# Second table in eight short steps; gated output projections made three per iteration, early in the attention loop

## The reference, cut to what matters

```python
mod = (silu(c) @ wmod).reshape(16, 6, 1, -1)     # sa, ca, ga, sb, cb, gb
ga, gb = sign(.) * maximum(abs(.), 0.25)
h = layernorm(x) * (1 + ca) + sa
x = x + ga * attention(h)     # 4 heads, two learned-slot tables of 64, causal, gated, then @ Wo
h = layernorm(x) * (1 + cb) + sb
x = x + gb * experts(h)       # layer norm, router, top 2 of 8 experts, 128 -> 512 -> gelu -> 128,
                              # weighted sum of the two, layer norm
```

## Time and profile before

| what | value |
|---|---|
| median of three runs | 498.81 us (498.32 to 500.5) |
| the profiled execution | 499.39 us |
| its span | 497.6 us |
| TensorE busy | 436.6 us, 88% |
| VectorE busy | 398.8 us, 80% |
| GpSimd busy | 347.0 us, 70% |
| ScalarE busy | 316.9 us, 64% |
| chain that ended last | TensorE 49%, GpSimd 23%, VectorE 16% |

### The profile page before, as it was taken

The page is one execution under the profiler, slowest core; times in us unless marked ns, Lnnn a source line. Parts: engine busy times, 40 slices in busy tenths (PEclk is TensorE's granted clock), DMA queues, the critical chain, the costliest instruction groups (busy, mean ns, idle before and its releaser), DMA issues.

```text
span 497.6 us, 11499 instructions
## 1 busy us (share of the span) xinstructions
PE 436.6 (88%) x3266; PEld 363.0 (73%) x3266; DVE 398.8 (80%) x1134; ACT 316.9 (64%) x813; POOL 347.0 (70%) x404
## 2 busy tenths in 40 slices
PE   3589999999899899899899766699889999999990
PEld 1366777776677677677677544599889999999980
DVE  2579999999989989989989975467677677786385
ACT  1166778888578678678688645565545555555574
POOL 4675865689979989989987546267567656665632
PEclk9999999999889889889999958599999999999996
DMA  6950000000000000000000050235434322226344
GB/s 152 236 160 0 7 8 5 2 18 19 25 17 19 23 19 19 24 17 19 24 22 14 18 193 23 54 75 175 148 91 105 90 72 69 73 65 229 118 137 125
DMA packets 33934, 33.66 MB, mean 68 GB/s; under 512 B 7037, under 2 KB 27681, under 8 KB 33745
## 3 DMA queue, kind: packets, MB, share of 16 engines
q1 hardware_dynamic: 27600, 22.39, 16.7%
q0 software_dynamic: 4320, 9.22, 5.5%
q10 hardware_dynamic: 1952, 1.32, 1.1%
HBM read 20.43 MB, written 12.48 MB: 66 GB/s over the span
## 4 chain that ended last, share of the span: by engine, by line
PE 49%; POOL 23%; DVE 16%; issue 6%; ACT 4%; DVEq 1%; DMA 0%; ACTq 0%; POOLq 0%
PE sa_ps L1625 12%; POOL xe_dram L388 8%; PE sa_ps L1635 6%; PE bank L1635 6%; PE sa_ps L1403 3%; POOL lgs L422 3%; POOL A_sb L395 3%; PE bank L1616 2%; POOL xn L473 2%; PE bank L1475 2%; POOL kT L445 2%; PE sa_ps L1396 2%; PE bank L1476 2%; PE bank L1600 2%; PE bank L1542 2%
## 5 line engine op out<-in xcount | busy, mean ns | idle before, releaser
L738 ACT ACTIVATE work<-sa_ps,work 128x128 f32<-128x128 f32 x284 | 81.0, 368 | 63.8 <-PE sa_ps L1625 61.9
L483 POOL DMA_INDIRECT y_dram<-work,idxr x71 | 72.4, 1020 | 44.8 <-DVE idxr L1203 32.4
L388 POOL DMA_INDIRECT xe_dram<-xrow,slot x64 | 72.6, 1134 | 24.5 <-issue 14.0
L1625 PE MATMUL sa_ps<-work 128*128 128x128 f32 x568 | 79.4, 284 | 0.0
L1625 PEld LDWEIGHTS sa_ps<-work 128*128 128x128 f32 x568 | 70.5, 195 | 0.2 <-DVE work L1210 0.2
L1403 PE MATMUL sa_ps<-Px,wvT 64*128 64x128 f32 (+1 forms) x288 | 41.4, 338 | 3.8 <-DVE Px L1106 3.7
L1403 PEld LDWEIGHTS sa_ps<-Px,wvT 64*128 64x128 f32 x288 | 33.7, 192 | 13.8 <-DVE Px L1106 9.2
L422 POOL TENSOR_TENSOR lgs<-lgs,rsum 128x256 f32<-128x256 f32 x32 | 30.6, 973 | 18.6 <-DVE rsum L1066 18.6
L1635 PE MATMUL bank<-w2s,work 128*128 x280 | 37.3, 276 | 2.7 <-DVE work L1245 2.7
L1635 PE MATMUL sa_ps<-w2s,work 128*128 x288 | 38.6, 278 | 0.9 <-DVE work L1245 0.6
L395 POOL TENSOR_SCALAR_AFFINE_SELECT A_sb<-A_sb 128x768 f32<-128x768 f32 (+1 forms) x32 | 19.9, 645 | 25.9 <-ACT A_sb L706 25.8
(11 more groups left out here) (280 smaller groups left out, 1119.8 us busy)
## 6 DMA issues: line engine op xcount, KB each, us to landing
work<-xe_dram SPq DMA_DIRECT2D x71, 69.5 KB
work<-in_w SPq DMA_DIRECT2D x1, 2048.0 KB, 9.8
outf<-outf_dram SPq DMA_DIRECT2D x1, 2048.0 KB, 9.8
xrow<-y_dram SPq DMA_DIRECT2D x4, 512.0 KB, 7.4
out<-x_sb SPq DMA_DIRECT2D x7, 256.0 KB, 2.6
y_dram<-work,idxr POOLq DMA_INDIRECT x71, 2.4
modb<-mod_dram SPq DMA_DIRECT2D x16, 64.0 KB, 2.8
xe_dram<-xrow,slot POOLq DMA_INDIRECT x64
```

What stands on the lines that cost most here:

```text
L388: nc.gpsimd.indirect_dma_start(xe_dram, bass.IndirectOffsetOnAxis(slot[:, 4 * batch + column:4 * batch + column + 1], 0), xrow[:, tile, :] ...
L483: nc.gpsimd.indirect_dma_start(y_dram, bass.IndirectOffsetOnAxis(idxr[:, n % RING["scat"]:n % RING["scat"] + 1], 0), y[:, n % RING["scat"] ...
L738: last = nc.scalar.activation(hid[:, n % 2, c, :], up_bank[n % 2][:, c * P:(c + 1) * P], ACT.Gelu, bias=w1c[:, n % 3, FF + c:FF + c + 1])
L1625: last = mm(up_bank[n % 2][:, c * P:(c + 1) * P], w1c[:, n % 3, c * P:(c + 1) * P], xgT[:, n % 3, :], start=True, stop=True)
```

## The change

- `Wob` gets 16 buffers of its own, one per batch, instead of two.
- GpSimd makes Wob at the head of its body, ahead of gate: in iteration 5 for batches 0 to 2, in iteration 6 for 3 to 5, and so on to iteration 9 (12 to 14), and in iteration 10 for 15. None is made in iterations 11 to 20 or behind the loop.
- The 17 operations of the second table are spread over eight steps, in `prepare` for n = 14, 16, ..., 28, and stand behind the register load of the next expert. The last operation of a step is marked and not waited for; the next step begins with a wait for it.
- The step of the gates that stood at n = 20 and 26 stands at 21 and 27.
- In the order written out by hand, TensorE's `turn(1)` stands ahead of the rank products of batch 13.

```diff
--- before.py
+++ after.py
@@ -122,7 +122,7 @@
         ss3, rs3 = sb("ss3", [P, 4, 2]), sb("rs3", [P, 4, 2])
         sq, rs, onT1, onT = sb("sq", [P, T]), sb("rs", [P, T]), sb("onT1", [P, T]), sb("onT", [P, 2, T])
         gate = sb("gate", [P, 4, T])
-        Wob = sb("Wob", [P, 2, D])
+        Wob = sb("Wob", [P, NB, D])
         xn2 = sb("xn2", [P, 2, 2, D])
         h2T = sb("h2T", [P, 2, T])
         sq3 = sb("sq3", [P, 2, D])
@@ -164,6 +164,7 @@
         PARTS = [(g, 0, GROUP) for g in range(NG - 1)] + [(NG - 1, 0, 2), (NG - 1, 2, 2)]
         DIAGONALS = range(36, 36 + 4 * NG, 4)
         AHEAD = 2 * (NB - 2)
+        LATE_STEPS = range(14, 30, 2)
         FACTORS = range(30, 30 + 2 * NB, 2)
         shapes = dict(w1s=[NE, FF + NC], xg=[RING["gath"], RW], xgT=[3, P], w1c=[3, FF + NC], hid=[2, NC * P], y=[RING["scat"], D])
         work = sb("work", [P, sum(n * m for n, m in shapes.values())])
@@ -404,15 +405,16 @@
             def iteration(i):
                 b = i - 5
                 if live(b):
+                    for ahead in range(3 * b, min(3 * b + 3, NB)):
+                        pool.wait_ge(S[f"modb_ld{ahead % 4}"], 16 * (ahead // 4 + 1))
+                        if ahead == 0:
+                            pool.wait_ge(S["vec_rdy"], 2)
+                        nc.gpsimd.tensor_tensor(Wob[:, ahead, :], Wog[:], modb[:, ahead % 4, :], ALU.mult).then_inc(S["wob_rdy"], 1)
+
+                b = i - 5
+                if live(b):
                     need(pool, "sig_rdy", b)
                     nc.gpsimd.tensor_tensor(gate[:, b % 4, :], g_sb[:, b % 2, :], eg[:, b % 2, :], ALU.mult).then_inc(S["gate_rdy"], 1)
-
-                b = i - 6
-                if live(b):
-                    pool.wait_ge(S[f"modb_ld{b % 4}"], 16 * (b // 4 + 1))
-                    if b == 0:
-                        pool.wait_ge(S["vec_rdy"], 2)
-                    nc.gpsimd.tensor_tensor(Wob[:, b % 2, :], Wog[:], modb[:, b % 4, :], ALU.mult).then_inc(S["wob_rdy"], 1)
 
                 b = i - 5
                 if live(b):
@@ -495,11 +497,6 @@
                                             compare_op=ALU.is_equal, fill=0.0, base=0, pattern=[[0, 2 * GROUP], [-1, P]], channel_multiplier=1).then_inc(S["diag_rdy"], 1)
 
             pipeline(iteration)
-            b = 15
-            pool.wait_ge(S[f"modb_ld{b % 4}"], 16 * (b // 4 + 1))
-            if b == 0:
-                pool.wait_ge(S["vec_rdy"], 2)
-            nc.gpsimd.tensor_tensor(Wob[:, b % 2, :], Wog[:], modb[:, b % 4, :], ALU.mult).then_inc(S["wob_rdy"], 1)
             b = 12
             need_group(pool, "slot_rdy", b)
             scatter(b, 0)
@@ -977,32 +974,36 @@
                 link(nc.vector.tensor_tensor(pv, pv, jump[:, 0:v].unsqueeze(2).broadcast_to([1, v, n]), ALU.mult))
                 link(nc.vector.tensor_reduce(row_f[:, 0:n], pv.rearrange("p e s -> p s e"), AX.X, ALU.add))
 
-            def late_counts():
-
-                link(nc.vector.tensor_scalar(early_i[:], early_i[:], 7, None, ALU.logical_shift_right))
-                link(nc.vector.tensor_scalar(count_i[:], count_i[:], 7, None, ALU.logical_shift_right))
-                nc.vector.tensor_copy(first[:, NE:2 * NE], early_i[:])
-                nc.vector.tensor_copy(ending[:, 0:NE], early_i[:])
-                link(nc.vector.tensor_copy(ending[:, NE:2 * NE], count_i[:]))
-
-            def late_bins():
-
-                link(nc.vector.tensor_tensor(ntile[:], ending[:], first[:, 0:2 * NE], ALU.subtract))
-                link(nc.vector.tensor_tensor_scan(tend[:], ones[0:1, 0:2 * NE], ntile[:], 0.0, ALU.mult, ALU.add))
-                link(nc.vector.scalar_tensor_tensor(out=jump[:], in0=first[:, 1:2 * NE + 1], scalar=float(REGION // P), in1=ending[:], op0=ALU.add, op1=ALU.subtract))
-                link(nc.vector.tensor_scalar(jump[:, NE - 1:NE], jump[:, NE - 1:NE], -float(PADROW // P), None, ALU.add))
-
-            def late_experts():
-
-                n = NS - NA
-                link(nc.vector.scalar_tensor_tensor(out=exp_f[:, 0:n], in0=past[:, (NE - 1) * n:NE * n], scalar=-float(NE), in1=exp_f[:, 0:n], op0=ALU.mult, op1=ALU.add))
-                link(nc.vector.tensor_scalar(exp_i[:, NA:NS], exp_f[:, 0:n], float(NE - 1), None, ALU.min))
-
-            def late_rows():
-
-                n = NS - NA
-                link(nc.vector.scalar_tensor_tensor(out=row_f[:, 0:n], in0=row_f[:, 0:n], scalar=first[:, 0:1], in1=iota_j[:, 0:n], op0=ALU.add, op1=ALU.add))
-                nc.vector.tensor_scalar(row_i[:, NA:NS], row_f[:, 0:n], float(P), None, ALU.mult).then_inc(S["table_rdy"], 1)
+            def late_step(k):
+
+                n, v = NS - NA, 2 * NE
+                pv = past[:, 0:v * n].rearrange("p (e s) -> p e s", e=v)
+                by_tile = pv.rearrange("p e s -> p s e")
+                if k == 0:
+                    link(nc.vector.tensor_scalar(early_i[:], early_i[:], 7, None, ALU.logical_shift_right))
+                    link(nc.vector.tensor_scalar(count_i[:], count_i[:], 7, None, ALU.logical_shift_right))
+                    nc.vector.tensor_copy(first[:, NE:2 * NE], early_i[:])
+                    nc.vector.tensor_copy(ending[:, 0:NE], early_i[:])
+                    mark(nc.vector.tensor_copy(ending[:, NE:2 * NE], count_i[:]))
+                if k == 1:
+                    link(nc.vector.tensor_tensor(ntile[:], ending[:], first[:, 0:2 * NE], ALU.subtract))
+                    nc.vector.tensor_tensor_scan(tend[:], ones[0:1, 0:2 * NE], ntile[:], 0.0, ALU.mult, ALU.add)
+                    link(nc.vector.scalar_tensor_tensor(out=jump[:], in0=first[:, 1:2 * NE + 1], scalar=float(REGION // P), in1=ending[:], op0=ALU.add, op1=ALU.subtract))
+                    mark(nc.vector.tensor_scalar(jump[:, NE - 1:NE], jump[:, NE - 1:NE], -float(PADROW // P), None, ALU.add))
+                if k == 2:
+                    mark(nc.vector.tensor_tensor(pv, iota_j[:, 0:n].unsqueeze(1).broadcast_to([1, v, n]), tend[:, 0:v].unsqueeze(2).broadcast_to([1, v, n]), ALU.is_ge))
+                if k == 3:
+                    mark(nc.vector.tensor_reduce(exp_f[:, 0:n], by_tile, AX.X, ALU.add))
+                if k == 4:
+                    link(nc.vector.scalar_tensor_tensor(out=exp_f[:, 0:n], in0=past[:, (NE - 1) * n:NE * n], scalar=-float(NE), in1=exp_f[:, 0:n], op0=ALU.mult, op1=ALU.add))
+                    mark(nc.vector.tensor_scalar(exp_i[:, NA:NS], exp_f[:, 0:n], float(NE - 1), None, ALU.min))
+                if k == 5:
+                    mark(nc.vector.tensor_tensor(pv, pv, jump[:, 0:v].unsqueeze(2).broadcast_to([1, v, n]), ALU.mult))
+                if k == 6:
+                    mark(nc.vector.tensor_reduce(row_f[:, 0:n], by_tile, AX.X, ALU.add))
+                if k == 7:
+                    link(nc.vector.scalar_tensor_tensor(out=row_f[:, 0:n], in0=row_f[:, 0:n], scalar=first[:, 0:1], in1=iota_j[:, 0:n], op0=ALU.add, op1=ALU.add))
+                    nc.vector.tensor_scalar(row_i[:, NA:NS], row_f[:, 0:n], float(P), None, ALU.mult).then_inc(S["table_rdy"], 1)
 
             def constants():
 
@@ -1208,23 +1209,14 @@
                    ALU.mult, ALU.add).then_inc(S["xgT_rdy"], 1)
                 need_tile(dve, "hid_rdy", n - 3)
                 nc.vector.tensor_copy(w1c[:, n % 3], w1s[:, bass.ds(e, 1), :].squeeze(1)).then_inc(S["w1c_rdy"], 1)
-                if n == 14:
-                    late_counts()
-                if n == 15:
-                    late_bins()
-                if n == 16:
-                    tile_bins(NS - NA, 2 * NE)
-                if n == 17:
-                    late_experts()
-                if n == 18:
-                    tile_rows(NS - NA, 2 * NE)
-                if n == 19:
-                    late_rows()
                 if n + 1 < NS:
                     chosen[n + 1] = expert(n + 1)
-                if n == 20:
+                if n in LATE_STEPS:
+                    dve.wait_ge(S["dve_chain"], chain[0])
+                    late_step(LATE_STEPS.index(n))
+                if n == 21:
                     tt(pw[:, AHEAD:NT, 0], top[:, AHEAD:NT, 1], top[:, AHEAD:NT, 0], ALU.subtract).then_inc(S["f_s0"], 1)
-                if n == 26:
+                if n == 27:
                     dve.wait_ge(S["f_s"], 2)
                     link(ts(gates[:, :, 0], pw[:, :, 1], 1.0, None, ALU.add))
                     link(nc.vector.reciprocal(gates[:, :, 0], gates[:, :, 0]))
@@ -1507,7 +1499,7 @@
                     need(pe, "wob_rdy", b)
                     need_groups_before(pe, "slot_rdy", b - 2)
                     for tile in range(2):
-                        last = mm(b7[:, tile * D:(tile + 1) * D], onT[:, b % 2, tile * P:(tile + 1) * P], Wob[:, b % 2, :], start=True, stop=True)
+                        last = mm(b7[:, tile * D:(tile + 1) * D], onT[:, b % 2, tile * P:(tile + 1) * P], Wob[:, b, :], start=True, stop=True)
                     last.then_inc(S["out_mm"], 1)
 
                 b = i - 3
@@ -1645,11 +1637,11 @@
```

(2 more changed lines are left out.)

## The result

The changed kernel takes 493.0 us (median of four runs, 492.1 to 494.06) against 499.65 of the kernel before, run beside it (four runs, 498.32 to 501.73): ratio 0.985 [0.982, 0.988]. That ratio makes 7.4 us less [6.0, 8.8]; the two medians alone lie 6.7 us apart. In a later comparison, beside 29 runs of the kernel before with a median of 501.17, the same kernel took 495.76 (six runs): ratio 0.989 [0.985, 0.992], 5.7 us less [3.8, 7.6]. It is faster by 1.1 to 1.5%, clear of the noise, and inside the range; the forecast of 3.0 us less was too small.

What follows compares the result with a forecast made beforehand. It took waits for VectorE's rsum and half-clocked TensorE, not GpSimd's own work, to bound much of the attention loop, and TensorE the expert stage. -4.2 + 1.8 - 0.6 + 0 = -3.0 from 498.81 gives 495.8 us, range 492.0 to 498.6.

Steps and rivals of the forecast that it cites:

- Second table, -4.2: Expert stage, four tiles taking 12.23 us instead of 8.0: eight spaced steps hide VectorE's extra work, 4.2 us less.
- The sum of lag per tile: VectorE in the old table tiles: addition 1.41, reduction 1.03, idle 0.85, at least 3.3 us against TensorE's 2.00.
- Three Wob per iteration, early, +1.8: GpSimd, iterations 5 to 9: extra early Wob delay rsum and lgs, 1.8 us more in all (0.8 to 3.3).
- The 0.4 forecast for iteration 5: Gate and last Wob move beside VectorE's two scans, rsum waits for them: +0.4 us (0 to 0.5).
- the 0.6 expected in iterations 6 and 9: Three Wob and gate make lgs late on the path: +0.6 us in each iteration (0.4 to 1.0).
- everything early is path: Rival, chance 0.14: early Wob in iterations 5 to 9 all count, 4.5 instead of 1.8 us; time 498.5.
- the strict reading: Shared ports as exclusive lock: every extra Wob holds VectorE up by its full length; time 498.5.
- No late Wob, -0.6: Iterations 11 to 20 and behind the loop: 0.14 in each of 12, 14, 16, perhaps 0.2 in 18; 0.6 us less.
- The prediction's own sign against it: Attention loop cycles shorter by 0.7 us or more would show the forecast wrong on the cause.
- turn(1), 0: Seam before turn(2): both orders reach TensorE's wait for VectorE's first xgT, 0 us (-0.3 to +0.3).
- Slower, by a clock that falls earlier: Rival, chance 0.06: longer TensorE idle in iterations 5 and 9 drops the clock twice, 3.0 us each; 501.8.
- priced a fall at 3.0 us: TensorE behind masked A_sb: seven groups take 8.06 us at half clock instead of 5.09, 3.0 us per fall.

Runs made afterwards that it cites:

- number 8: Kernel before, table still in six consecutive tiles, but next expert's register load ahead of each step and its last operation not waited for: 499.17 against 501.25, ratio 0.995.
- 9: Kernel before with the table in eight spaced steps, but the register load behind each step and its last operation waited for: 497.6 against 501.44, ratio 0.993.
- number 6: Changed kernel with its three Wob ahead of GpSimd's wait for the copied A_sb, not ahead of gate: 495.58, ratio 0.990 to the kernel before.
- number 5: Changed kernel with the late Wob made again into a spare tile, iterations 11 to 20 and behind the loop: 495.88, ratio 0.989 to the kernel before.
- number 4: The changed kernel run again without an edit (the repeat), beside the kernel before: 495.76 against 501.17, ratio 0.989.
- number 3: Kernel before with only turn(1) moved ahead of the rank products of batch 13: 500.52 against 501.17, ratio 0.998.
- number 7: Changed kernel with three overwritten matmuls ahead of TensorE's wait for masked A_sb in iterations 10, 12, 14, 16: 488.68 against 501.25 of the kernel before, ratio 0.975.
- number 10: Kernel before with its single Wob per iteration ahead of gate instead of behind it: 500.53 against 501.44, ratio 0.998.
- number 2: Kernel before with only the Wob part: three per iteration, early, each with its own buffer: 499.74 against 501.17, ratio 0.997.
- number 11: As number 7, with more overwritten matmuls in iterations 19 and 20, ahead of Px in 19 and of turn(2): 486.45 against 501.44, ratio 0.968.

## Why the prediction was right or wrong

*Direction and range: right.* 493.0 lies in 492.0 to 498.6. The size was too small by 2.7 us in the second comparison and by 4.4 in the first. Of the three terms only the table's stands as it was summed; the term of the early Wob was mis-sized, and the part on Wob as a whole came out with the other sign.

*Second table, -4.2: right in place and size.* 4.24 us gained in the four tiles named, 3.7 us as measured alone, and the reductions are gone from the chain. The cause that the prediction gave was double, short steps on every second tile and a load that runs ahead of a step whose end isn't waited for. The second is enough (number 8). The sum of lag per tile, 1.41 + 1.03 + 0.85 = 3.3 us against 2.00, was right as arithmetic; without the 0.85 even a tile with 0.67 and 1.03 us of extra work (number 8) stays within the lag that TensorE forgives. Which of the two, the load's place or the unwaited end, does it isn't told apart: numbers 8 and 9 move both.

*Three Wob per iteration, early, +1.8: the step that failed.* It was mis-sized: by the lgs starts it is 0.2 us (61.78 against 61.57, and against 61.55 in number 6). The other profiles have 61.54 to 61.77 us here with the old loop and 61.77 to 61.83 with the early Wob. The 0.4 forecast for iteration 5 isn't there either, as the scans of 1.26 us show. The prediction took 0.83 us per Wob from the single Wob of the earlier trace rows, a row that lies beside a scan. Three in a row took 1.76 us at the same place, 0.59 each, and VectorE's pair of scans in iteration 6 took 1.47 us beside them, not the 1.74 of the earlier trace rows. Where GpSimd had waited 0.85 us for rsum, the two extra Wob lie now: three Wob and gate take 2.6 us there, and gate, Wob and the wait took 2.5. So neither rsum nor lgs moved by the 0.6 expected in iterations 6 and 9. The rival "everything early is path", +4.5, falls with it. By the Trainium skill ("SBUF — State Buffer", section "SBUF: two separate sides") the two engines hold their shared ports for whole instructions. The trace agrees in direction (three Wob take 1.27 us beside a light VectorE, 1.76 beside its scans); the strict reading, every Wob at its full length on VectorE, gave 498.5, and the runs exclude that time.

*No late Wob, -0.6: no gain seen*, by number 5, whose noise is larger than 0.6. The reading behind it, that only 0.14 of the 0.71 us was GpSimd's own, was right; the chain's 23% for GpSimd would have misled a reader who hadn't looked at VectorE's timeline. The cycle is 36.94 us where the forecast said 36.8. The prediction's own sign against it, a cycle shorter by 0.7 or more, came up once (36.25 instead of 37.01 us from iteration 14 to 16 in the first profile) and not in the repeat (37.20). It goes with the shorter stretch of half clock shown in number 4.

*turn(1), 0: right* (number 3).

*What the sum didn't have.* Two things. The step from iteration 10 to 11 is 18.47 us after and 19.30 before, 0.83 less, in the first profile and in the repeat. Timeline of VectorE there, first the kernel before, then the changed one:

```profile
131.60 2.00 DVE L929 TENSOR_TENSOR onehot<-iota_e,xrow 128x64 bf16<-128x64 f32 x1
133.63 0.62 DVE L933 TENSOR_TENSOR_SCAN seen<-keep,onehot 128x72 bf16<-128x72 bf16 x1
...
134.75 1.30 DVE L900 TENSOR_SCALAR wkT<-wkT 128x512 f32<-128x512 f32 x1
```

```profile
132.16 0.23 DVE L926 TENSOR_TENSOR onehot<-iota_e,xrow 128x64 bf16<-128x64 f32 x1
132.43 1.88 DVE L930 TENSOR_TENSOR_SCAN seen<-keep,onehot 128x72 bf16<-128x72 bf16 x1
...
134.81 0.54 DVE L897 TENSOR_SCALAR wkT<-wkT 128x512 f32<-128x512 f32 x1
```

The same three operations meet GpSimd in other places. The long one ends 0.1 to 0.2 us behind the end of GpSimd's causal mask of A_sb in both (the mask ends at 133.51 and at 134.14 us). The length of the clip wkT goes with the step: 0.54 us with steps of 18.45 and 18.47 (number 8 and the changed kernel), 0.66 with 18.67 (number 7), 1.07 with 19.09 (number 10), 1.30 with 19.30 (the kernel before). Number 6, whose Wob lie elsewhere, doesn't fit: 1.60 with 18.11. Of the six profiles with the old loop five have 19.09 to 19.31 us here, and number 8 has 18.45; the six with the Wob early ahead of gate have 18.46 to 18.67. So the change makes the short pattern likely, but the old loop can fall into it as well; number 10 shows that order alone doesn't bring it. Why it does so stays open. This is 0.8 of the 1.4 us of number 2; the remaining 0.6 lies within its interval. The second thing is the granted clock: at the end of the loop 0.76 in the first profile and 0.68 in that of number 4, 1.9 us that a repeat didn't have, and some 1.3 us more behind iterations 14 and 16. That is luck of an execution. It may be part of why the first comparison gave 7.4 us and the second 5.7, whose intervals overlap.

*Slower, by a clock that falls earlier: no.* TensorE idled 1.32 us in iteration 5 and kept its 2.4 GHz. That rival took it that the idle time decides, between 1.12 and 1.59 us. The runs don't bear that out: with the same 1.50 or 1.51 us of idle in iteration 16 the clock fell in eight profiles and stayed up in three (the first of the changed kernel among them).

## What to carry to other kernels

Put a register load that depends on a finished table ahead of operations whose end is waited for: the wait cost 0.85 us in each such tile here, and moving the load, with the last wait taken out, was worth as much as the whole respacing. Read an engine's share of the chain together with the timeline of what it waits for; 11 points of the chain changed hands and the cycle stayed at 36.9 us. Look at the granted clock before counting instructions: three wasted matmuls in an idle time of 1.6 us, in four iterations, were worth some 7 us, about as much as the whole change. And look at it in two executions before putting a difference down to an edit: the loop was 3.1 us shorter in the first profile of the changed kernel and 0.3 in the second.

## What the runs showed of the hardware

- Behind an idle time of 1.59 us the granted clock fell to the 1.2 GHz level (0.56 in 171.20 to 178.00), and with 0.28 us in its place it stayed at 2.4 GHz (1.00 in 134 to 246, number 7). But the idle time before one instruction doesn't settle it: 1.50 or 1.51 us in iteration 16 did both, and in number 11 the clock fell behind 0.22 and 1.06 us (0.66 in 208 to 213).
- The prediction priced a fall at 3.0 us; a pair of iterations without it is 1.3 us shorter. The rest was probably hidden behind VectorE, which now is busy 107.53 of 112.00 us; no run shows that by itself.
- The Trainium skill ("TensorE: Matmul & The Clock Gate", section "HAM oscillation — how this bites in real kernels") describes falls behind long waits for DMA. Its section "A second HAM failure mode: psum-queue depth-cycling" describes falls from small, frequent idle times between groups of matmuls. The idle time of 1.59 us here is neither: it waits for GpSimd's mask, in one piece, once per 37 us.
- A VectorE operation that meets GpSimd can grow by some 1.8 us: the comparison for onehot took 0.23 or 2.00 us, the scan behind it 1.88 or 0.62 (0.46 in number 6). Which of the two is hit decides little; whether a second is hit (wkT, 0.54 or 1.30) decides 0.8 us.
